# Two-layer gated transformer block: the shared expert moved in among the routed experts, the routing round reordered

## The reference

```python
x = hidden_states.reshape(-1, h)                      # the normalised input
shared = silu(x @ shared_wg.T) * (x @ shared_wu.T) @ shared_wd.T
scores = sigmoid(x @ gate_w.T)
topw, topi = top_k(scores, 8)
topw = topw / topw.sum(-1, keepdims=True)
# pos: the how-manyeth token of its expert each choice is
buf = zeros((64, 256, 256)).at[e_flat, pos].set(xin, mode='drop')
g = silu(einsum('ech,eih->eci', buf, expert_wg))
u = einsum('ech,eih->eci', buf, expert_wu)
out_buf = einsum('eci,ehi->ech', g * u, expert_wd)
routed = (out_buf[e_flat, pos].reshape(T, K, h) * topw[..., None]).sum(1)
# outside:  x = x + tanh(g_ffn[1]) * (shared + routed)
```

## Time and profile before

| what | us |
|---|---|
| median of 3 timed runs | 2313.06 |
| the three runs | 2312.68, 2313.06, 2321.97 |
| the profiled execution, its own time | 2309.97 |
| its span | 2308.1 |
| routing stage, first instruction to the first gather | 1627.99 to 1848.51 |
| of it the seven round starts, select(0) to select(7) | 1649.42 to 1811.76 |
| experts, first gather to the last scatter's landing | 1848.51 to about 2269.6 |
| end, loads of the two planes to the end of the span | 2269.64 to 2308.1 |

### The profile page before, as it was taken

The page is one execution under the profiler, slowest core; times in us unless marked ns, Lnnn a source line. Parts: engine busy times, 40 slices in busy tenths (PEclk is TensorE's granted clock), DMA queues, the critical chain, the costliest instruction groups (busy, mean ns, idle before and its releaser), DMA issues. The chain is left out here.

```text
span 2308.1 us, 52796 instructions
## 1 busy us (share of the span) xinstructions
PE 1738.1 (75%) x22308; PEld 1329.5 (58%) x22308; DVE 1258.5 (55%) x2416; ACT 793.1 (34%) x1420; POOL 656.3 (28%) x594
## 2 busy tenths in 40 slices
PE   5999999379564889888889887795566576677665
PEld 3777776268543667666667665674344354455443
DVE  5766666267332768666776677684477521111113
ACT  2555554133131443344334433342165411111110
POOL 2121211067420110021011101101000078888882
PEclk9999999689875788778878877787677589988896
DMA  6787875213245123322322232101122156565567
GB/s 139 151 153 139 145 139 96 78 64 101 62 133 110 47 75 57 66 66 74 66 60 70 67 76 42 43 21 29 61 71 81 45 143 129 116 135 121 124 123 237
DMA packets 224844, 216.79 MB, mean 94 GB/s; under 512 B 62724, under 2 KB 200430, under 8 KB 224096
## 3 DMA queue, kind: packets, MB, share of 16 engines
q1 hardware_dynamic: 194080, 179.01, 32.9%
q0 software_dynamic: 24576, 27.05, 6.9%
q10 hardware_dynamic: 5952, 7.35, 0.9%
HBM read 147.08 MB, written 72.45 MB: 95 GB/s over the span
## 5 line engine op out<-in xcount | busy, mean ns | idle before, releaser
L2128 DVE TENSOR_TENSOR e_hT<-e_sil,e_ps_gu 128x256 f32<-128x256 f32 x64 | 26.9, 421 | 323.4 <-ACT e_sil L2150 323.4
L1316 DVE TENSOR_TENSOR r_score<-r_ps_s,r_score 128x512 f32<-128x512 f32 x256 | 172.2, 689 | 47.1 <-PE r_ps_s L1566 42.9
L2157 ACT ACTIVATE e_y<-e_ps_y,k_rows 128x256 f32<-128x256 f32 x128 | 53.7, 471 | 323.3 <-DMA base_scratch<-e_y,k_token 162.4
L1535 PE MATMUL r_ps_s<-r_q,r_rk 96*128 96x64 bf16 x2048 | 148.6, 236 | 20.3 <-DMA r_q<-parts_scratch 13.0
L1176 POOL TENSOR_TENSOR r_avT<-r_avT,r_w 128x1024 f32<-128x1024 f32 x16 | 37.7, 2355 | 439.4 <-DMA r_w<-r_w_raw 439.4
L2092 POOL DMA_INDIRECT k_rows<-rows_w_scratch,k_token x128 | 135.0, 1055 | 90.7 <-issue 90.4
L1286 DVE TENSOR_TENSOR r_score<-r_score,r_ps_t 128x1024 f32<-128x1024 f32 x128 | 154.2, 1215 | 10.6 <-PE r_ps_t L1546 9.9
L332 DVE TENSOR_REDUCE a_row_max<-a_ps_max 128x2 f32<-128x512 f32 (+1 forms) x192 | 130.3, 685 | 53.1 <-PE a_ps_max L482 28.7
L1535 PEld LDWEIGHTS r_ps_s<-r_q,r_rk 96*128 96x128 bf16 x2048 | 128.0, 120 | 48.1 <-issue 20.3
L1406 ACT ACTIVATE r_score<-r_ps_s 128x512 f32<-128x512 f32 x192 | 111.5, 601 | 113.0 <-PE r_ps_s L1535 111.8
L1566 PE MATMUL r_ps_s<-r_q,r_k 96*128 96x64 bf16 x2048 | 115.0, 203 | 46.3 <-DMA r_k<-parts_scratch 32.1
(11 more groups left out here) (299 smaller groups left out, 4163.4 us busy)
## 6 DMA issues: line engine op xcount, KB each, us to landing
a_q<-parts_scratch SPq DMA_DIRECT2D x96, 128.0 KB, 4.2
a_k<-parts_scratch SPq DMA_DIRECT2D x96, 128.0 KB, 7.0
r_q<-parts_scratch SPq DMA_DIRECT2D x96, 128.0 KB, 3.1
e_wg<-in_L_ffn_expert_wg SPq DMA_DIRECT2D x64, 128.0 KB, 2.4
e_wu<-in_L_ffn_expert_wu SPq DMA_DIRECT2D x64, 128.0 KB, 3.1
e_wd<-in_L_ffn_expert_wd SPq DMA_DIRECT2D x64, 128.0 KB, 3.4
r_k<-parts_scratch SPq DMA_DIRECT2D x4, 1536.0 KB, 14.3
rows_w_scratch<-m_row SPq DMA_DIRECT2D x8, 640.0 KB, 3.2
```

What stands on the lines that cost most here:

```text
L1316: dve.tensor_tensor(part, ps_s[c % 2][:].rearrange("p (c e q) -> p c q e", c=4, e=2), part, ALU.add).then_inc(added, 1)
L1535: ins = pe.matmul(ps_s[c % 2][:, n * BH:(n + 1) * BH], rk6[:, j:j + P], q_now[:, :, q, :], start=True, stop=True)
```

## The change

1. **Last step of relative attention.** Of the 16 moves of `w2_raw`, 8 stay on SP and 8 are issued by ACT.
2. **Routing.** The shared expert leaves the round: no up products, no silu (and so no table loads between exponential and silu), no `hT`, no down product, no `x_base`, no write of `base_scratch`. DVE normalises right after the moments; `clamp(r+1)` stands between the two digit comparisons of round r. The load of the next input waits on a normalisation rather than on `x_base`. Before the rounds, moments and normalisation of round 0 come ahead of the three constants that wait for `gate`; PE no longer waits for those constants. In the last round DVE makes the four copies by the tile's number.
3. **Experts.** The even plane is `x3` itself, which the layer's input is in. The shared expert runs in 16 groups of 256 tokens, one per four experts: SP loads 256 normalised rows, PE turns them in the expert with e % 4 = 1, makes the up products at e % 4 = 2 and the down product at the next e % 4 = 0; DVE copies and multiplies, ACT takes the silu and copies the result to `own_y`, which stays in SBUF.
4. **End.** POOL adds `own_y` to the odd plane's buffer before DVE adds the two planes; DVE waits for it.

```diff
@@ relative_attention, SP and ACT
-                    for j in range(4):
+                    for j in range(4 if front else 2):
...
+                if back and not front:
+                    act.wait_ge(w2_copied, START + 2 * h + 2)
+                    for j in range(2, 4):
+                        for q in range(4):
+                            act.dma_start(w2[32 * j:32 * j + DH, q], w2_raw[32 * q:32 * q + DH, j]).then_inc(w2_moved, 16)
@@ expert_ffn
-    sums = [base.rearrange("b s d -> (b s) d"), slots_in[0:T]]
+    sums = [x3.rearrange("b s d -> (b s) d"), slots_in[0:T]]
@@ routing, SP
-                    sp.wait_ge(base_ready, START + 2 * r)
+                    sp.wait_ge(xn_ready, START + r * G)
...
-                sp.wait_ge(base_ready, START + 2 * r + 2)
-                sp.dma_start(base_rows[r], x_base[:]).then_inc(base_written, 16)
@@ routing, VectorE
             take_moments(0)
             normalise(0)
+            dve.wait_ge(const_loaded, START + 16 * 5)
...
             for r in range(R):
                 select(r)
                 if r + 1 < R:
                     take_moments(r + 1)
-                dve.wait_ge(sil_ready, START + r + 1)
-                dve.wait_ge(gu_ready, START + 2 * r + 2)
-                dve.wait_ge(y_ready, START + 2 * r)
-                dve.tensor_tensor(hT[:], sil[:], ps_gu[1][:], ALU.mult).then_inc(h_ready, 1)
-                if r + 1 < R:
                     normalise(r + 1)
                 count_round(r)
                 weigh(r)
-                dve.wait_ge(base_written, START + r * 16)
-                for n in range(2):
...
-                    dve.wait_ge(y_ready, START + 2 * r + n + 1)
-                    dve.tensor_tensor(x_base[:, half, :].rearrange("p g d -> p (g d)"),
...
+                take_high(r)
                 if r + 1 < R:
                     clamp(r + 1)
-                take_digits(r)
+                take_low(r)
+            for t in range(G):
+                dve.wait_ge(low_ready, START + (R - 1) * G + t + 1)
+                dve.tensor_scalar(value[:, t, :, K16:2 * K16, :], at_low[:, t], float((R - 1) * G + t), None, ALU.mult)\
+                    .then_inc(tile_ready, 1)
@@ experts, POOL behind its last wait for the scatters
+            pool.wait_ge(own_y_copied, START + SHARED)
+            for r in range(R):
+                pool.wait_ge(sums_loaded[r % NB], START + 32 * (r // NB + 1))
+                pool.tensor_tensor(sum1[r % NB][:].rearrange("p g d -> p (g d)"), sum1[r % NB][:].rearrange("p g d -> p (g d)"),
+                                   own_y[:, 2 * r:2 * r + 2].rearrange("p s c d -> p (s c d)"), ALU.add).then_inc(own_added, 1)
@@ experts, VectorE at the end
                 dve.wait_ge(sums_loaded[r % NB], START + 32 * (r // NB + 1))
+                dve.wait_ge(own_added, START + r + 1)
@@ experts, ScalarE between silu(e) and y(e-1)
+                if e and e % EVERY == 0:
+                    s = e // EVERY - 1
+                    act.wait_ge(own_y_ready, START + s + 1)
+                    act.activation(own_y[:, s].rearrange("p c d -> p (c d)"), ps_own[:], ACT.Copy).then_inc(own_y_copied, 1)
+                if e < E and e % EVERY == 2:
+                    act.wait_ge(own_gu_ready, START + e // EVERY + 1)
+                    act.wait_ge(own_h_ready, START + e // EVERY)
+                    act.activation(own_sil[:], ps_own[:, 0:CAP], ACT.Silu).then_inc(own_sil_ready, 1)
@@ experts, TensorE
                 up_gate(e)
                 down(e - 1)
+                if e % EVERY == 0:
+                    own_down(e // EVERY - 1)
+                if e % EVERY == 1:
+                    own_turn(e // EVERY)
+                if e % EVERY == 2:
+                    own_up_gate(e // EVERY)
```

More of the change, by code:

```diff
@@ L1974, in take_logits @@
                 ins.then_inc(gated, 1)
[L1976 to L1982 removed]
             turn(0)
+            pe.wait_ge(const_loaded, START + 16 * 5)
             take_logits(0)
[L1986 removed]
             for r in range(R):
@@ L1996, in _ @@
                 ins.then_inc(counted, 1)
[L1997 to L2006 removed]
+                if r + 1 < R:
+                    turn(r + 1)
+                    pe.wait_ge(weight_ready, START + r + 1)
+                    take_logits(r + 1)
                 pe.wait_ge(late_ready, START + r + 1)
@@ L2044, in expert_ffn @@
         y_last = sb("y_last", [E, D], F32)
+        SHARED = T // CAP
+        EVERY = E // SHARED
+        own_rows = [sb(f"own_rows{i}", [P, C, D], F32) for i in range(2)]
+        own_xT, own_sil, own_hT = sb("own_xT", [P, ND * CAP], F32), sb("own_sil", [P, CAP], F32), sb("own_hT", [I, CAP], F32)
+        own_y = sb("own_y", [P, SHARED, C, D], F32)
         NB = 4
```

111 lines of the change are left out of this document (58 added, 53 removed).

## The result

The changed kernel takes 2277.87 us, median of three runs (2277.11 to 2278.89), against 2313.06: a ratio of 0.983, with a 95% interval of 0.981 to 0.986. That is 35.2 us faster by the medians and 32.9 by the spans of the two profiled executions (2308.1 and 2275.2), where 42 were summed. The time lies 8 us above the forecast and inside the range.

A forecast was written before the change was run, and what follows sets the result against it. It took GpSimd's descriptor writing to bound the experts, VectorE the rounds, DMA the end and SP's issuing the moves. Terms -5.0, -3.0, -30.2, -7.3, +0.5, +3.0 sum to -42.0: 2268 or 2271, predicted 2270 us, range 2256 to 2290.

The forecast's parts named there:

- The moves: Last step of relative attention: SP issues 8 moves instead of 16 while ScalarE issues the other 8; -5.0 us.
- the start: Start of the routing: moments, normalisation and turn come earlier, no longer behind constants that wait for `gate`; -3.0 us.
- the rounds: Seven routing rounds: 18.3 us each plus 4.1 for the memsets, 132.2 against 162.4; -30.2 us.
- the hold by the memsets: Routing, behind GpSimd's last root: clearing the row buffers slows VectorE's normalisation beginning together with it; charged 4.1 us.
- the rival of the map's loop: Rounds: the circle of low comparison, copies, map products, counts and clamp holds them at 20 us; time 2280; chance 0.12.
- dropped at no gain: Writes of `base_scratch` and the silu's table loads, waited for only through `x_base` and `hT`: no gain of their own.
- Three of its signs: Expected: end within 5 us of 38.5, experts' span within 1 us of before, scatters still waiting on issue alone.
- The step that was mis-sized in the last round: Last select to last map product: 27.9 us becomes 20.6, with ScalarE dropping four of eight copies; -7.3 us.
- The part besides the copies: Last round, select to the end of `at_high`, with the counts waiting for round 6's map: 14.9 us after the change.
- The step that was mis-sized at the end: End: GpSimd's eight adds lie under DMA-bound loads, except the last pair passes one more engine; +3 us.
- The exclusion rival: End: GpSimd's adds hold VectorE's, first store 9.4 us later, end +11.8 us; time 2277; chance 0.08.
- Experts: Expert stage: shared groups fit in TensorE's idle time, at most 71 us in 136; 0.5 us charged for the first expert.

## Why the prediction came out as it did

**What was right.** The moves (-4.7, forecast -5.0), the start (-3.3, -3.0) and the rounds (-32.0, -30.2) each came out within 2 us in the profiled pair, and undoing the moves, the start's order and the clamp's place brought their time back in their stage alone. In the rounds both reasons held: round length without the memsets is 126.7/7 = 18.1 us (forecast 18.3), the clamp waits 0.52 us (forecast up to 0.55), and the hold by the memsets costs 3.7 (forecast 4.1). The counts were waited for in the last round only, so the rival of the map's loop, with 20 us a round, did not occur, although its margin was under 1 us. What the prediction called dropped at no gain (the silu's table loads, the writes of `base_scratch`) has no row of its own in the result, and no run tested it apart. Three of its signs came out just beyond what it named: the end is 5.9 us longer (within 5), the experts 1.1 (within 1), and the scatters wait 3.0 us for ScalarE, not on issue alone. Two of VectorE's eight final adds are stretched (3.29 and 2.06 us); the other six take 1.2.

**The step that was mis-sized in the last round.** Forecast -7.3, measured -5.4. The part besides the copies was put at 3.4 and measured 28.0 - 24.0 = 4.0. The copies were put at 3.9, and gave 1.4 in the changed kernel. The step took ScalarE's eight copies as the limit and the map products as following them; with the operands early, TensorE's own pause of 2.67 us came last, probably a load of its instructions.

**The step that was mis-sized at the end.** Forecast +3, measured +5.9 in this pair of executions, and about 5 by all of them. The step had two parts. One was right in kind: the last pair passes one more engine, put at 2.4 or a little more, measured 3.3 with the last GpSimd add stretched to 3.13 us. The other was put at almost nothing: that the eight adds lie under the loads. But the last pair landed 2.6 us later than before, so the loads were not free of the adds; that the reused buffers carry this delay is likely and not shown. The exclusion rival gave +11.8. Half of that came, but a like end came with the adds on VectorE too, where no add was stretched. The rows show the stretching that this rival named, but not the 9.4 us by which it put the first store back: that store is issued 10.1 us behind the first load (2240.95 - 2230.82), and was at 7.5 before the change, so it is 2.7 later.

**Experts.** Forecast +0.5; the kernel without groups says 0 to 2, which the scatter doesn't resolve. ScalarE's waiting covered the groups: in front of the copies to `e_y` it still waits 303.0 us in all, where it was 323.3. TensorE's share was 37.4 us, where the prediction allowed up to 71.

**What the sum left out.** -38.2 us came from the stretches that the change touches. In the profiled pair 5.3 of it were hidden by relative attention, which ended later with unchanged code. The sum's 2268 against the profiled run's 2277.11 is thus these 5.3 and 3.8 us of mis-sized terms (the end costs 2.9 more and the last round gains 1.9 less than forecast, the start and the rounds together gain 2.1 more, and the rest makes 1.1). That the errors of the terms partly cancel is luck, and so is the sign of the 5.3. The changed kernel's second set of runs had a median of 2274.79.

## What to carry over

When work leaves a serial loop, look at which wait is last once it is gone, and move an independent step into that hole: here the work that left gave 15.5 us or more and the one moved line 16.5. At a DMA-paced end, count the work between landing and store, not only the engine on which it runs, and above all on the last pair, where nothing covers it; adding to an operand that was already in SBUF cost nothing here that shows (37.6 and 40.5 us, as without the adds). Compare stages by their own lengths, from start to start: two single executions of the kernels here differ by up to 15 us before the first changed instruction.

## What was not expected of the hardware

TensorE paused for 2.67 us after 165 of 256 small products (128x32, bf16), and went on 2.28 us after the last operand was there. In the ten other executions with the shared copies it stopped at the same product, for 1.87 to 2.43 us. The profile names no wait for it; a 16 KB packet of instructions, described above, overlaps every one of these stops.

In the seven rounds TensorE's granted clock was 0.71 before the change, with TensorE busy for 110.8 of 162.4 us, and 0.53 after it, with 66.9 of 130.4: nearly all of the time at the lower of its two levels, 1.2 GHz. The clamp waits for logits that are made there.

The contention between GpSimd and VectorE reached both ways at the end: 3.29 us for a VectorE add of 1.23, and 3.33 for a GpSimd add of 2.35. In the routing GpSimd's memsets held a VectorE instruction of 0.41 us for 4.12 us, as long as all seven memsets took (4.07).

Unchanged code ahead of the change ended between 1594.3 and 1609.2 us in fourteen executions. Most of that arises in relative attention. From its first to its last copy to `w_raw` it took 777.4 us in the one execution with a granted clock of 0.83 there, 780.8 to 789.7 in seven at 0.82, and 786.6 to 790.6 in six at 0.81. So the longer executions tend to have the lower clock; why it differs is open.
